# A graph attention layer on one core: x1 steps, scores, table products and low parts of the weights at other places

## What is computed

```python
x1 = relu(x @ W_ah + b_ah)
for W, a_s, a_d, b in layers:                       # three layers
    h = (x1 @ W).reshape(N, H, C)
    as_n = (h * a_src).sum(-1)
    ad_n = (h * a_dst).sum(-1)
    e = leaky_relu(as_n[src] + ad_n[dst], 0.2)
    m = segment_max(e, dst)
    p = exp(e - m[dst])
    alpha = p / (segment_sum(p, dst)[dst] + 1e-16)
    out = segment_sum(alpha[:, :, None] * h[src], dst)
    xs.append(relu(out.reshape(N, H * C) + b))
y = relu(concatenate(xs, axis=1) @ W_out + b_out)
return layernorm(x + y)
```

## Time and profile before

| | us |
|---|---|
| median of 3 runs | 1026.37 |
| lowest, highest | 1024.56, 1026.64 |
| the profiled execution | 1024.96 |
| its span in the profile | 1023.3 |
| TensorE busy | 968.4 (95%) |
| VectorE busy | 759.9 (74%) |
| ScalarE busy | 364.9 (36%) |

### The profile page before, as it was taken

How to read it: one execution, slowest core, us unless ns; L and a number is a source line. 1 busy time by engine, 2 the same in 40 slices (tenths; PEclk the granted TensorE clock), 3 DMA queues, 4 the chain that set the end, 5 groups by cost and what they waited for, 6 DMA issues and landing times. The chain is left out here.

```text
span 1023.3 us, 14393 instructions
## 1 busy us (share of the span) xinstructions
PE 968.4 (95%) x5560; PEld 896.9 (88%) x5560; DVE 759.9 (74%) x1055; ACT 364.9 (36%) x524; POOL 22.0 (2%) x34
## 2 busy tenths in 40 slices
PE   5799995899999988999999999999999999999996
PEld 2577752699999988999999999999999959999996
DVE  5699996663999986999898998997988364324322
ACT  1245530212212214445636555555455281001000
POOL 1000000000000000000001001001000010000000
PEclk9899997899999998999999999999999999999998
DMA  5331071323444327122615335315822163323201
GB/s 192 97 83 36 1 235 43 105 90 110 160 157 132 111 96 211 51 88 59 142 50 129 71 88 126 88 38 177 314 63 88 39 174 126 136 78 101 81 31 31
DMA packets 60889, 108.10 MB, mean 106 GB/s; under 512 B 17212, under 2 KB 44445, under 8 KB 59686
## 3 DMA queue, kind: packets, MB, share of 16 engines
q1 hardware_dynamic: 43700, 66.36, 21.4%
q0 software_dynamic: 4048, 18.60, 7.2%
q10 hardware_dynamic: 13090, 22.44, 6.9%
HBM read 80.31 MB, written 27.08 MB: 105 GB/s over the span
## 5 line engine op out<-in xcount | busy, mean ns | idle before, releaser
L1230 PE MATMUL ps<-R_W 125*125 125x193 f32 x2400 | 400.4, 329 | 6.9 <-DVE R_W L939 4.2
L1230 PEld LDWEIGHTS ps<-R_W 125*125 125x125 f32 x2400 | 393.9, 189 | 10.5 <-ACT R_XIN L672 6.0
L657 ACT ACTIVATE R_W<-R_EXP,s 125x1250 f32<-125x1250 f32 x120 | 161.2, 1344 | 166.8 <-PE ps L1230 114.6
L939 DVE SCALAR_TENSOR_TENSOR R_W<-R_W,R_CNT 125x1250 f32<-125x1250 f32 x120 | 174.7, 1456 | 3.9 <-DVE R_EXP L928 2.0
L898 DVE CUSTOM_DVE_ANT_0 R_ROWS<-R_MASK,R_ROWS 125x1250 bf16<-125x1250 bf16 x100 | 138.5, 1458 | 0.7 <-ACTq L610 0.7
L1190 PE MATMUL ps<-Wl_hi,x_hi 128*125 128x384 f32 x360 | 123.7, 344 | 0.0
L1190 PE MATMUL ps<-Wl_lo,x_hi 128*125 128x384 f32 x360 | 123.2, 342 | 0.0
L1190 PE MATMUL ps<-Wl_hi,x_lo 128*125 128x384 f32 x360 | 123.2, 342 | 0.0
L1301 PE MATMUL ps<-Wo_hi,xs_hi 128*125 128x384 f32 x324 | 109.5, 338 | 0.3 <-PE ps L1279 0.3
L1301 PE MATMUL ps<-Wo_lo,xs_hi 128*125 128x384 f32 x324 | 109.2, 337 | 0.0
L1301 PE MATMUL ps<-Wo_hi,xs_lo 128*125 128x384 f32 x324 | 109.2, 337 | 0.0
(11 more groups left out here) (143 smaller groups left out, 801.8 us busy)
## 6 DMA issues: line engine op xcount, KB each, us to landing
xs_dram<-R_XIN POOLq DMA_DIRECT2D x18, 625.0 KB, 9.3
h_dram<-R_HOUT ACTq DMA_DIRECT2D x30, 336.0 KB
R_W<-h_dram SPq DMA_DIRECT2D x12, 840.0 KB
R_ROWS<-as_dram SPq DMA_DIRECT2D x12, 625.0 KB, 3.7
R_EXP<-u_dram SPq DMA_DIRECT2D x6, 1250.0 KB, 6.4
R_X<-u_dram SPq DMA_DIRECT2D x6, 1250.0 KB, 5.8
R_ROWS<-in_W_all SPq DMA_DIRECT2D x18, 384.0 KB, 3.6
Wo_sb<-in_W_out POOLq DMA_DIRECT2D x1, 6912.0 KB, 27.8
```

What stands on the lines that cost most here:

```text
L657: nc.scalar.activation(prob[r % PSLOTS], expo[:, r % XSLOTS], ACT.Exp, bias=s02[:, r % NT, ds(2 * p + r // NT, 1)]).then_inc(S["exp_done"], 1)
L939: nc.vector.scalar_tensor_tensor(out=prob[r % PSLOTS], in0=prob[r % PSLOTS], scalar=HUGE, in1=cntT[:, r % NT], op0=ALU.min, op1=ALU.mult). ...
L1230: ins = mm(ps[0:PT, o:o + HW], prob[r % PSLOTS][:, t * PT:(t + 1) * PT], hB[:, q, j], start=(j == 0 and t % 2 == 0), stop=(j == NT - 1), s ...
```

## The change

- **Start.** The loads for `V` wait until the second part of `xT` is in; one block of `V` instead of two stands before the windows; two x1 steps instead of six stand before the transposes. ScalarE issues windows 5 to 7 behind its first x1 evacuation. The batches are cut otherwise, and no weights are loaded between them.
- **Window loop.** Three x1 steps per four windows instead of four.
- **Scores.** All six blocks behind the last x1 step.
- **Extra count.** 15 of the 18 products of the second tile of half table 0 stand inside the loop of `more_counts`, between the counts and the mask block ("table products first").
- **Low parts.** Those of half tables 1 to 5 stand inside heads 0, 2, 4, 6 and 8, at tile 8.
- **End of the layer products.** The shifts are transposed behind tile 2 instead of 6 of the last half table; the first two exponentials stand behind its tiles 7 and 8 instead of one behind tile 8.

```diff
-BATCHES = [(0, 2), (2, 8), (8, 18), (18, 28), (28, 38), (38, NW)]
+BATCHES = [(0, 2), (2, 8), (8, 14), (14, 22), (22, 32), (32, 42), (42, NW)]
+ACT_SLOTS = (5, 8)
-V_HEAD = 2
+V_HEAD = 1
-SCORES_AT = 15
-U_AT = 6
+U_AT = 2
+EXP_AT = NT - 3
...
 def x1_upto(w):
-    return min(X1_HEAD + w + 1, X1_STEPS)
+    return X1_HEAD + 3 * (w + 1) // 4
...
+            sp.wait_ge(x0_in[G0_PARTS - 2], 16)
             load_a(0)
...
-                with sp.Fori(w0, w1) as w:
+                with sp.Fori(w0, min(w1, ACT_SLOTS[0]) if i == 1 else w1) as w:
...
+            x1_out(0)
+            act.wait_ge(S["table_sb"], 1)
+            with act.Fori(*ACT_SLOTS) as w:
+                start = act.value_load(table[0:1, ds(w, 1)], min_val=0, max_val=EDGES)
+                act.dma_start(e8[:, ds(w, 1)].rearrange("p o s i -> p (o s) i"),
+                              edges[:, ds(start, SLOT)].rearrange("s (p i) -> p s i", i=CPW)).then_inc(win_in[1], 16)
...
-                    if n == PARTS - 1 and t == NT - 2:
-                        exp_tile(0, 0)
+                    if n == PARTS - 1 and t - EXP_AT in (0, 1):
+                        exp_tile(0, t - EXP_AT)
...
-            rest_w(1)
...
-                    if b == 5 and hh % 2 == 1 and (hh + 3) // 2 < PARTS:
-                        rest_w((hh + 3) // 2)
+                    if b == NT - 2 and hh % 2 == 0:
+                        rest_w(hh // 2 + 1)
...
-            for s in range(KT):
+            for s in range(KT // G0_PARTS):
                 x1_step(s)
             pe.wait_ge(S["reach_sb"], 1)
...
             for s in range(half_way, X1_STEPS):
                 x1_step(s)
-                if s == KT * SCORES_AT + KT - 1:
-                    pe.wait_ge(S["mask_ready"], 2 * NT)
-                    pe.wait_ge(S["v_made"], 2 * HEADS * KT * LAYERS)
-                    for k in range(KT // 2):
-                        scores(k)
-            for k in range(KT // 2, KT):
+            pe.wait_ge(S["mask_ready"], 2 * NT)
+            pe.wait_ge(S["v_made"], 2 * HEADS * KT * LAYERS)
+            for k in range(KT):
                 scores(k)
...
                         edge_products(bank(7)[0:PT, 256:256 + MC], ones_more, True, True).then_inc(S["more_ps"], 1)
+                        h_products(0, 1, range(KT - 1))
                         pe.wait_ge(S["more_stage"], nth + 1)
...
+                    first = KT - 1 if n == 0 and t == 1 else 0
+                    h_products(n, t, range(first, KT)).then_inc(S["h_ps"], 1)
```

More of the change, by code:

```diff
@@ L338, in _ @@
                                  edges[:, ds(start, SLOT)].rearrange("s (p i) -> p s i", i=CPW)).then_inc(win_in[i], 16)
[L339 to L342, removed]
             for l in range(LAYERS):
-                for k in range(V_HEAD + VSLOTS if l == 0 else 0, KT):
+                for k in range(V_HEAD if l == 0 else 0, KT):
                     load_v(l, k)
+                    if (l, k) == (0, VSLOTS):
+                        load_a(1)
                     if (l, k) == (1, VSLOTS):
@@ L566, in _ @@
             act.wait_ge(S["small_in"], 32)
-            for i in range(X1_HEAD // KT):
+            x1_out(0)
[4 more added lines that the diff above has]
+                              edges[:, ds(start, SLOT)].rearrange("s (p i) -> p s i", i=CPW)).then_inc(win_in[1], 16)
+            for i in range(1, X1_HEAD // KT):
                 x1_out(i)
@@ L708, in round_wo @@
                 nc.scalar.copy(Wo_hi[:, k], Wo_sb[:, k]).then_inc(S["wo_hi"], 1)
-            for r in range(1, NT):
+            for r in range(2, NT):
                 exp_tile(0, r)
@@ L1113, in _ @@
             mm(bank(3)[0:1, NW:2 * NW], ab[:, 2:3], ident[0:NW, 0:NW], start=True, stop=True).then_inc(S["rows_ps"], 1)
-            for s in range(KT, X1_HEAD):
+            for s in range(KT // G0_PARTS, X1_HEAD):
                 x1_step(s)
@@ L1142, in _, with h_products @@
                 x1_step(s)
-                if s == KT * SCORES_AT + KT - 1:
-                    pe.wait_ge(S["mask_ready"], 2 * NT)
-                    pe.wait_ge(S["v_made"], 2 * HEADS * KT * LAYERS)
-                    for k in range(KT // 2):
-                        scores(k)
-            for k in range(KT // 2, KT):
-                scores(k)
+            pe.wait_ge(S["mask_ready"], 2 * NT)
+            pe.wait_ge(S["v_made"], 2 * HEADS * KT * LAYERS)
+            for k in range(KT):
+                scores(k)
+            def h_products(n, t, blocks):
+                place = bank((2 * (n % 2) + t) % 4)[0:PT, 0:HALF]
+                for k in blocks:
+                    if n == 0 and t == 0:
+                        pe.wait_ge(S["x1_lo"], k + 1)
+                        pe.wait_ge(S["w_lo"], 1)
+                    for i, (xx, ww) in enumerate(((x1_hi, Wl_hi), (x1_hi, Wl_lo), (x1_lo, Wl_hi))):
+                        ins = mm(place, xx[:, k, t * PT:(t + 1) * PT], ww[n][:, k],
+                                 start=(k == 0 and i == 0), stop=(k == blocks[-1] and i == 2), skip_group_check=True)
+                return ins
             def scores_turn():
@@ L1162, in more_counts @@
                 more, each = passes(pe)
+                pe.wait_ge(S["h_sb"], 2)
                 with pe.Fori(0, more) as t:
@@ L1178, in h_part @@
             def h_part(n):
-                c = n % 2
                 pe.wait_ge(S["w_hi"], n + 1)
@@ L1184, in h_part @@
                     pe.wait_ge(S["h_sb"], NT * n + t + 1)
-                    for k in range(KT):
-                        if n == 0 and t == 0:
-                            pe.wait_ge(S["x1_lo"], k + 1)
-                            pe.wait_ge(S["w_lo"], 1)
-                        for i, (xx, ww) in enumerate(((x1_hi, Wl_hi), (x1_hi, Wl_lo), (x1_lo, Wl_hi))):
-                            ins = mm(bank((2 * c + t) % 4)[0:PT, 0:HALF], xx[:, k, t * PT:(t + 1) * PT], ww[n][:, k],
-                                     start=(k == 0 and i == 0), stop=(k == KT - 1 and i == 2))
-                    ins.then_inc(S["h_ps"], 1)
+                    first = KT - 1 if n == 0 and t == 1 else 0
+                    h_products(n, t, range(first, KT)).then_inc(S["h_ps"], 1)
                     if n == 0 and t == 0:
```

## The result

The changed kernel takes 990.0 us (median of 4 executions, 988.48 to 991.97) against 1026.36 (1024.56 to 1026.64) beside it: a ratio of 0.965, 95% interval 0.9626 to 0.9675. In a later comparison it took 991.75 (989.03 to 992.46, 5 executions), ratio 0.9653 [0.9638, 0.9667]. The forecast was 992.8, range 986 to 1004. The profiled execution took 991.97 with a span of 990.3, against 1024.96 and 1023.3: 33.0 us less, where the sum said 33.6.

What follows compares the result with a forecast made beforehand. TensorE, busy 95%, was taken as the bound, with gains only where it idles or runs at 1.2 GHz. 17.2 + 4.6 + 6.3 + 3.5 + 2.0 = 33.6 us gave 992.8 against the median 1026.37; range 986 to 1004.

Steps and rivals of the forecast that it cites:

- Start: First window loads: VectorE's first batch at 17.8 instead of 21.10 us, second at about 25.2, 4.7 us sooner.
- Window loop: 48 windows: VectorE sets the pace with three x1 steps per four windows; loop ends at 116.6 instead of 127.4 us.
- the term of 1.6 us for windows at the lower clock: Window loop: 1.6 us added for windows that meet TensorE at its lower clock after the batch wait.
- signs of a wrong forecast: Granted clock under 1.00 in the window loop, or TensorE waiting for `V` or for the shifts.
- so the two hold each other up: Old window loop: TensorE needs 1.96 us a window at wide x1 tiles, VectorE 1.84, together taking 2.03 each.
- V, x1 and scores: Before the layer products: `V` ends at 156.0, x1 at 155.9, scores take 12.8; layer products at 169.5, 17.2 us sooner.
- the 169 to 171 that were to show the forecast right: Sign of a right forecast: the layer products begin from 169 to 171 us.
- Extra count: Counting stage after the layer products start: 4.6 us saved at full clock, 2 if one 1.47 us idle stretch lowers the clock.
- Low parts and shifts: End of layer products: VectorE's shifts ready at T + 170.7, TensorE there at T + 172.4; 6.3 us saved, 1.7 margin.
- Rival 1: VectorE late to the shifts, TensorE stalls 2 to 4 us: 1002.8 us; chance 0.18 together with the second rival.
- Start of attention: From shifts to first attention product: seven tiles cover the 4.15 us wait, 0.6 to 0.7 left; 3.5 us saved.
- The last term: Start of the attention stage: the stretch 398 to 402 us at clock 0.50 runs at full clock, 2.0 us saved.

Runs made afterwards that it cites:

- again: The changed kernel itself, nothing altered, profiled a second time in the later comparison: 991.75 us, ratio 0.9653.
- start_old: Changed kernel with the old start: six x1 steps before the transposes, two V blocks first, loads not held back, all window loads on SyncE; 999.71 us, 0.9741.
- x1_four: Changed kernel with four x1 steps per four windows again instead of three: 994.81 us, ratio 0.9702.
- x1_two: Changed kernel with two x1 steps per four windows instead of three: 997.78 us, ratio 0.9722.
- layer_alone: Kernel before the change with only the low parts, shifts and exponentials moved as in the change: 1015.6 us, ratio 0.9887.
- low_new_u6: Changed kernel, low parts at their new places, but shifts behind tile 6 and one exponential ahead as before: 997.77 us, ratio 0.9714.
- low_old_u6: Changed kernel with low parts, shifts (behind tile 6) and first exponential all at their old places: 1002.52 us, ratio 0.9766.
- sync_alone: Changed kernel with all window loads issued by SyncE again, none by ScalarE, rest of the new start kept: 995.76 us, ratio 0.9703.
- fill_more: Changed kernel with six products of the second tile ahead of the extra count and 15 of the third tile inside it: 988.31 us, ratio 0.9628.

## Why the prediction came out

**Start.** Right: 17.65 and 23.55 for 17.8 and 25.2. In the first profile the second is 1.65 us better, since ScalarE issued its first load at 17.85, between its first two evacuations, and not from 20.0; the limit is then VectorE's own work on `table`. In again ScalarE issued from 20.16 and the batch began at 24.96, close to the forecast. Undersized was what the start is worth: 4.7 us of it went into the sum, start_old shows 7.9 at T, because 1.65 more was gained and the windows behind the late batch ran at a lower clock (0.82 over 17 to 46 us).

**Window loop.** Right at the end: 116.6 was forecast and 116.0 measured. In the first profile the loop took 92.5 us from 23.55 on for a forecast 91.4, in again 90.8 from 24.96 on (to 115.80), so there both parts came out as forecast. The difference of the two has the size of the term of 1.6 us for windows at the lower clock: from the second batch to the last group it is 79.4 us at a clock of 0.94 and 77.8 at 1.00. A granted clock under 1.00 in the window loop stood among the signs of a wrong forecast; it was there, 0.80 from 26 to 30 and 0.78 from 30 to 34 us in the first profile, but only behind the batch wait.

The weak step is "so the two hold each other up". From the second batch to the start of `V` VectorE took 97.5 us before (127.4 - 29.93), 93.7 in start_old (123.93 - 30.24), 93.2 in x1_four (116.98 - 23.80) and 92.5 in the changed kernel. The four-step pace costs VectorE 0.7 us by the last two, 2.3 at the same clock, and not the 4 to 7 of the expectation. Of the 5.0 us between the first and the last number, 3.8 are there with the start of before too: the 3.15 us wait for the third batch is gone, and the pace has its share; how the rest divides can't be told from profiles of different clocks (0.88, 0.82, 1.00 and 0.94 over 17 to 46 us). The forecast came out because all of these were in its one sum. That the loads' order alone takes the 3.15 us away was not tried; the batches are cut otherwise too.

**V, x1 and scores.** Right: `V` at 155.6 for 156.0, x1 at 155.8 for 155.9, scores 12.77 for 12.8, T at 168.5 for 169.5. The layer products thus began a little before the 169 to 171 that were to show the forecast right. Here lies the larger worth of the new pace: without it TensorE idles 7.53 us and the scores take 2.8 us longer, and T is 3.6 us later. The forecast had both in it, the idle stretch as filled with x1 steps and the clock by taking twice the fast half of the scores, 12.8 where before it was 7.95 + 6.41.

**Extra count.** Forecast 4.6 at full clock, or 2 if one idle stretch sufficed for the lower clock. It did suffice in the profiled execution, and still 3.8 us were gained: the tile behind tile 1 begins at T + 12.0, before at T + 15.8. The term mis-sized is the price of the fall: it lasted for ten products, not for the tile. In x1_four, x1_two and low_new_u6 the clock did not fall there; in the first two the way to the attention stage is 1.5 us shorter, and not 2.6. At full clock the gain is thus 5.3, more than the forecast; its own terms (7.2 + 2.6 + 0.6 + 0.5) end at T + 10.9 and not at the T + 11.2 it went on with.

**Low parts and shifts.** Right: the wait of 3.65 us is gone, the margin is 1.57 us for a forecast 1.7, and VectorE meets the low parts with waits of 0 to 1.5 us, all for ScalarE's rounded part (L591). Rival 1 did not come in.

**Start of attention.** By the sum's terms it starts at T + 211.2 - 14.4 = T + 196.8; it was T + 197.5, of which 0.8 is the extra count. The 3.5 us came (0.77 of idle time is left). The last term was 2.0 us for products at full instead of half clock from 398 to 402. The clock is now 1.00, and 196 products were done in the first 32 us instead of 180, but from the first attention product to the end it takes 624.3 us instead of 625.3: **1.0 us**, not 2.0. At least part of the rest is given back: TensorE waits longer for ScalarE's `R_XIN` in this stage. The waits of the changed kernel and of the one before (us in total, times, longest):

```profile
PE ps L1239 <- ACT R_XIN L678: 3.5, 7, 1.1
```

```profile
PE ps L1230 <- ACT R_XIN L672: 2.3, 8, 0.3
```

The first is of 360 to 620 us, the second of the whole span; over the whole span the changed kernel has the 3.9 of the page's row above. The stretches behind the start of attention:

```profile
366.00:398.00 32.00, 31.96 (x196) 31.99 (x197) 31.20 (x25) 15.95 (x12) 0.00 (x0) 1.00 0.30 93
398.00:568.00 170.00, 167.05 (x1037) 165.40 (x1037) 158.93 (x141) 90.03 (x119) 5.86 (x6) 1.00 0.37 89
```

In 170 us TensorE idles 2.95 us, where before it idled 1.37 (430 to 600 us). Every kernel that starts the stage after 0.77 us of idle time takes 624.2 to 624.3 us from there, layer_alone among them; low_new_u6, with 6.07 ahead, takes 625.3 like the kernel before. With 5.21 ahead, low_old_u6 takes 624.8. So the term is 0.5 to 1.0 us, by what lies ahead. That VectorE, busy for 93% here, takes back the rest of the lead is argued, not shown.

**The sum** in the profiles: 18.3 to T (forecast 17.2), 13.7 from there to the attention stage (14.4), 1.0 behind it (2.0), together 33.0 (33.6); the errors cancel in part by chance. Behind T the parts add up: undoing them costs 4.25 (count) and 9.8 (low parts and shifts, 375.80 - 168.49 - 197.54), 14.0 for the 13.7. Ahead of T undoing them costs 7.9 (start), 10.3 (scores) and 3.6 (pace), 21.8 for 18.3. That each has its full effect only while the other two keep the ends of x1 and `V` together would explain the surplus, but it is not shown: T differs by 1.5 us between profiles of the same code, and by 2.6 for the code of before.

## What to carry to other kernels

When two engines must meet at one point, give the freely movable work to the place where it makes both arrive at once; the even pace of a loop matters less than what is left over behind it. Price an idle stretch of TensorE with what follows it: here the scores behind 7.53 us of idle time took 2.8 us more than their 12.8, and a batch 3.0 us late, with a lower clock behind it, cost 4.2. And move a producer and its consumer together: the earlier shifts alone cost 5 us, the earlier low parts alone gained half.

## What the runs showed of the hardware

- **An idle stretch of 1.1 us can go either way.** The changed kernel's executions lie at 988.5 to 989.0 us with a mean clock of 0.999, or at 991.4 to 992.5 with 0.995 or 0.996. Before the second comparison I expected none in between, and there was none. Behind an idle stretch of 1.10 to 1.12 us in the extra count the clock fell in both profiles of the changed kernel (products of 0.52 us) and in six more, start_old and sync_alone among them (to attention 197.55 and 197.56); it did not fall in x1_four, x1_two and low_new_u6 (to attention 196.03 and 196.04 in the first two, so 1.5 us). The other part is in the start: from the second batch to the last group it is 79.4 us with a clock of 0.94 over 17 to 46 us and 77.8 with 1.00, so 1.6 us; T is 168.50 there and 167.44 in fill_more. In again the clock is 1.00, but the first x1 products are slow and the second batch late, and T is 168.28. These 1.5 and 1.6 us are together about the distance of the two levels. What decides it is open; fill_more, without the stretch, still has executions 2.2 us apart.
- **Many short gaps do not bring the lower clock.** With 8.11 us of gaps in 72 us of window loop (x1_two) it stays at 1.00. The page "TensorE: Matmul & The Clock Gate" of the Trainium skill, section "A second HAM failure mode: psum-queue depth-cycling", tells of micro-idles between groups of products that bring the clock down. These did not.
